# Graph attention, mix and experts on one core: table counts, first edge maxima and the exponentials of k moved into the projections

## The chip, the cores and the metric

The kernel runs on one core of a Trainium2 chip, as one launch. The metric is the device time of that launch in microseconds (us); lower is better. Executions of the kernel before took 1727.99, 1735.38 and 1739.04 us.

## What is computed

x has 1250 nodes of 768 features; the graph has 21,250 edges and a loop at each node. Three parts follow each other: a graph network, a linear attention ("the mix") and a mixture of experts. All inputs of the first two come from LayerNorm(x) or a first linear layer of it.

```
gat_conv (3 layers, H = 4 heads, C = 192):
    h = (x1 @ W).reshape(N, H, C)
    e = leaky_relu((h * a_src).sum(-1)[src] + (h * a_dst).sum(-1)[dst], 0.2)
    m = segment_max(e, dst);  p = exp(e - m[dst]);  s = segment_sum(p, dst)
    out = segment_sum((p / s[dst])[:, :, None] * h[src], dst)
mix (12 heads of 64, 256 features):
    data_dash = (64 ** -0.25 * data) @ proj.T
    q' = ratio * (exp(data_dash - diag - max over its own features) + EPS)
    k' = ratio * (exp(data_dash - diag - max over all heads, nodes, features) + EPS)
    out = q' (k'^T v) / (q' . sum k')
```

What matters for the change: the maximum under the exponential of k is one number over everything, so k' can't be finished before the last product of k is known; and the softmax over edges is worked densely, on a table of 1250 x 1250 counts (how often an edge u to v occurs), so that no edge is gathered.

## The kernel before

**Order.** A generator, `whole_order`, yields all steps of the program as one list cut into ticks, and each engine runs its own part of each step in that order (SP issues most of the DMAs, POOL the scatters). The engines are held together by semaphores only. `paced` lets tracks run side by side: a track with rate 0.5 puts one of its steps into every second tick. Within the second part two tracks of rate 1 run side by side: `projection_steps` followed by `mix_steps`, and `graph_steps`.

**First part.** LayerNorm, the first linear layer (x1) and h of three layers on TensorE. Meanwhile VectorE makes, in groups of eight chunks, the places and amounts of 170 chunks of 125 edges, and POOL (`place_`, L2043) adds each chunk into a table in DRAM with an indirect DMA. There are two tables, used in turn, because a scatter must wait until the last one into the same table has landed. Both are filled with zeros at the start (L2018).

**Projections** (`projection_steps`). v is made in 20 ticks; then come 36 products in two ticks each: for each of six pairs of heads the k rows (n even, c = 0 to 2) and the q rows (n odd), in columns of 512, 512 and 226. One half of a product is nine matmuls. During the q products of a pair `k_top` (L968, L1366) forms data_dash of that pair's k, tile by tile (three matmuls of 512 columns, `dash_into`, into banks 4 and 5 in turn), and VectorE takes its maximum. The product is then thrown away. `qk_split` puts k and q as two bf16 parts into an SBUF row, and `qk_store` writes it to DRAM. top_max, top_turn and top_spread give the maximum of all to every partition, and k_shift = -(diag + top).

**Graph** (`graph_steps`). It waits until the projections are over. Then come the counts (rate 0.6 a tick, ten tiles): SP loads a row block of both tables (L2155), VectorE adds them and the loops (L1387), ScalarE copies to bf16, TensorE transposes it (`count_turn`, L985), and VectorE makes `absent` (L1396), -3e38 where there is no edge. Then the 40 `edge_max` steps of layer 0 (L1408, rate 1.1 a tick; four heads x ten tiles), and `shifts` (L1418), which goes through DRAM to be spread to all partitions by `head_in` (L2187). Only then the attention begins: 120 items at 0.5 a tick, each `edge_z` (VectorE), `edge_exp` (ScalarE), `weigh` (VectorE), `gather` (20 matmuls, TensorE); beside it the 80 edge maxima of layers 1 and 2 at 0.6 a tick.

**Mix** (`mix_steps`). For each of six pairs 10 ticks of k tiles, 10 of q tiles, 3 empty ones: `dash` (L1018, three matmuls), then for k `k_exp` (L1887: two Exp with bias k_shift, and a Relu that adds EPS) and `k_sum` (L1027), for q `q_exp`, `q_turn`, `q_feat`, `q_out`, `divide`. After it come the output products of the mix and of the three layers (`row_block`), each layer's as soon as its attention is through, then the experts.

The waits that the prediction speaks of, before the change:

```
pe.wait_ge("k_max", i - 1)                # k_top(i): the maximum two tiles back is taken
sy.wait_ge("scatter0", 16 * (CHUNKS - CHUNKS // TABLES))   # SP, first load of a table: all scatters
ve.wait_ge(f"shift_in{lh % 2}", 32 * (lh // 2 + 1))        # edge_z: head_in's rows have landed
ve.wait_ge("gather_mm", i - EDGE_BUFFERS + 1)
```

## Time and profile before

| | us |
|---|---|
| three runs | 1727.99, 1735.38, 1739.04 (median 1735.38) |
| profiled execution | 1733.43 |
| its span, from the first to the last instruction | 1731.7 |
| TensorE busy (matmuls) in the span | 1569.7 (91%) |
| VectorE busy | 1121.2 (65%) |
| ScalarE busy | 682.0 (39%) |
| POOL busy | 411.0 (24%) |

The profile is of one execution. The span leaves out 1.7 us of the execution's own time. Busy times are unions of instructions; a matmul's end is modelled, and a busy TensorE can still issue faster or slower, so rates are read from the starts of successive instructions. PEclk is the share of full speed that TensorE's clock was granted.

### The profile page before, as it was taken

Reading aid. Unit: us, or ns where it says so; the run is one execution under the profiler, and the core shown is the slowest. Engines: PE = TensorE matmul, PEld = TensorE weight load, DVE = VectorE, ACT = ScalarE, POOL = GpSimd, SP = SyncE. Lnnn points to the kernel's source line nnn. Section 1 sums busy time; section 2 is a strip of 40 time slices with the busy share of each in tenths; the row PEclk is TensorE's granted clock in tenths of the full one; section 3 lists DMA queues with packets and bytes.
Section 4 is the critical chain, followed back from the end, with each engine's and each line's share of the span. In section 5 each row is a group of like instructions: output and inputs, shape, how many; then the busy total and the mean of one; then the engine's idle time right before and its main releaser. Section 6 shows DMA issues by size and latency. Waiting matters only on the chain.

```text
span 1731.7 us, 24915 instructions
## 1 busy us (share of the span) xinstructions
PE 1569.7 (91%) x9670; PEld 1195.3 (69%) x9731; DVE 1121.2 (65%) x2563; ACT 682.0 (39%) x1359; POOL 411.0 (24%) x250
## 2 busy tenths in 40 slices
PE   3979999999997888799999899989999999986987
PEld 2556666556654666689888788878889886665664
DVE  6678664114343597878778999968667753885233
ACT  4421000122222776667777543446334522441110
POOL 3777777768740000000000000000000000002331
PEclk9999999999998998899999899998999999996999
DMA  9234534453522422514212534444123214645951
GB/s 345 21 66 112 118 82 112 70 100 56 130 52 104 161 90 77 170 35 141 76 38 80 186 112 148 140 164 142 63 80 111 96 40 145 229 178 193 319 156 53
DMA packets 192568, 207.41 MB, mean 120 GB/s; under 512 B 80801, under 2 KB 149039, under 8 KB 192450
## 3 DMA queue, kind: packets, MB, share of 16 engines
q1 hardware_dynamic: 116354, 183.88, 32.2%
q0 software_dynamic: 75232, 19.57, 7.7%
q10 hardware_dynamic: 864, 2.36, 0.4%
q8 instruction: 77, 1.26, 0.3%
q14 instruction: 41, 0.34, 0.1%
HBM read 141.62 MB, written 65.27 MB: 119 GB/s over the span
## 4 chain that ended last, share of the span: by engine, by line
PE 74%; DVE 14%; ACT 5%; DMA 3%; issue 3%; SPq 1%; POOLq 0%; POOL 0%; ACTq 0%; DVEq 0%
PE bank L1012 19%; PE bank L858 13%; PE bank L859 13%; PE bank L857 12%; PE bank L1181 4%; PE bank L1169 3%; PE bank L1037 2%; DVE junk L1414 2%; PE bank L1065 2%; DVE eb L1451 2%; DVE eb L1460 1%; ACT ef L1883 1%; PE bank L959 1%; PE bank L1080 1%; DVE q_max L1483 1%
## 5 line engine op out<-in xcount | busy, mean ns | idle before, releaser
L1012 PE MATMUL bank<-hb,eb 128*128 128x193 f32 (+3 forms) x2400 | 419.7, 332 | 26.8 <-DVE eb L1460 21.8
L1012 PEld LDWEIGHTS bank<-hb,eb 128*128 128x128 f32 (+3 forms) x2400 | 401.1, 191 | 37.9 <-DVE eb L1460 24.8
L2049 POOL DMA_INDIRECT table<-amount,place x170 | 347.2, 2042 | 120.8 <-DMA table<-amount,place 71.9
L2055 POOL IOTA iota8i<- 128x8 int32 x1 | 0.1, 140 | 940.9 <-DMA node_rows<-node 940.9
L1844 ACT ACTIVATE eb<-eb,asd 128x640 f32<-128x640 f32 (+1 forms) x240 | 181.6, 812 | 54.9 <-DVE eb L1451 54.9
L1451 DVE SCALAR_TENSOR_TENSOR eb<-shift_b,as_low,shift_b 128x640 f32<-128x640 f32 (+1 forms) x240 | 196.3, 859 | 6.9 <-DMA shift_b<-shift_rows 6.8
L1460 DVE SCALAR_TENSOR_TENSOR eb<-eb,count 128x1280 f32<-128x1280 f32 (+1 forms) x120 | 174.3, 1453 | 6.4 <-ACT eb L1844 6.2
L1414 DVE CUSTOM_DVE_ANT_0 junk<-ab,absent 128x1250 bf16<-128x1250 f32 x120 | 174.3, 1453 | 1.3
L857 PE MATMUL bank<-wg_hi,x1T_hi 128*128 128x384 bf16 (+3 forms) x360 | 118.7, 330 | 0.5 <-DVE x1T_lo L1283 0.5
L857 PE MATMUL bank<-w_o_hi,aT_hi 128*128 128x384 bf16 (+1 forms) x360 | 118.6, 330 | 0.0
L859 PE MATMUL bank<-w_o_hi,aT_lo 128*128 128x384 bf16 (+1 forms) x360 | 118.5, 329 | 0.0
L859 PE MATMUL bank<-wg_hi,x1T_lo 128*128 128x384 bf16 (+3 forms) x360 | 118.5, 329 | 0.0
L858 PE MATMUL bank<-wg_lo,x1T_hi 128*128 128x384 bf16 (+3 forms) x360 | 118.5, 329 | 0.0
L858 PE MATMUL bank<-w_o_lo,aT_hi 128*128 128x384 bf16 (+1 forms) x360 | 118.5, 329 | 0.0
L1297 DVE TENSOR_TENSOR h_row<-bank,bgr 128x384 f32<-128x384 f32 (+1 forms) x60 | 32.4, 555 | 64.5 <-PE bank L859 64.3
L1883 ACT ACTIVATE ef<-bank,q_shift 128x256 f32<-128x256 f32 (+1 forms) x120 | 50.6, 477 | 59.8 <-DVE q_shift L1488 59.7
L858 PE MATMUL bank<-xnT_lo,wq_hi 128*128 128x512 bf16 (+1 forms) x210 | 70.8, 337 | 3.5 <-DVE wq_lo L1259 2.7
L859 PE MATMUL bank<-xnT_hi,wq_lo 128*128 128x512 bf16 (+1 forms) x216 | 73.0, 338 | 0.3
L1716 DVE TENSOR_TENSOR orow<-bank,b2r 105x384 f32<-105x384 f32 (+1 forms) x32 | 17.8, 555 | 84.5 <-PE bank L1181 84.5
L1369 DVE TENSOR_REDUCE kmax<-bank 128x1 f32<-128x512 f32 (+1 forms) x60 | 40.2, 692 | 49.1 <-PE bank L859 49.1
L1824 ACT ACTIVATE sq<-bank 128x512 f32<-128x512 f32 (+1 forms) x36 | 18.7, 519 | 130.0 <-PE bank L859 130.0
L857 PE MATMUL bank<-xnT_hi,wq_hi 128*128 128x512 bf16 (+1 forms) x204 | 68.6, 336 | 0.0
(286 smaller groups left out, 2945.8 us busy)
## 6 DMA issues: line engine op xcount, KB each, us to landing
w<-in_w SPq DMA_DIRECT2D x16, 1152.0 KB, 12.6
shift_b<-shift_rows SPq DMA_DIRECT2D x24, 625.0 KB, 5.9
h_rows<-h_row SPq DMA_DIRECT2D x27, 388.0 KB
hb<-h_rows SPq DMA_DIRECT2D x12, 873.0 KB
ar<-node_rows SPq DMA_DIRECT2D x27, 384.0 KB, 3.2
qk_rows<-qk_row SPq DMA_DIRECT2D x12, 625.0 KB
ab<-as_rows SPq DMA_DIRECT2D x12, 625.0 KB, 5.8
stage<-in_W SPq DMA_DIRECT2D x18, 384.0 KB, 4.2
```

What stands on the lines that cost most here:

```text
L857: T.matmul(out_ap, lhs[0], rhs[0], start=first, stop=False, skip_group_check=skip)
L858: T.matmul(out_ap, lhs[0], rhs[1], start=False, stop=False, skip_group_check=skip)
L859: return T.matmul(out_ap, lhs[1], rhs[0], start=False, stop=last, skip_group_check=skip)
L1012: ins = T.matmul(bank[w // 2][0:M, c0:c0 + GC + 1], p[0:K, u, w * P:w * P + M], hv[0:K, t, 0:GC + 1], start=opens and u == 0 and w % 2 == ...
L1169: ins = T.matmul(bank[i % 2][:, 0:CAP], w1s[e % WEIGHT_SETS][:, k, f * 128:(f + 1) * 128], sT_of(k)[:, e * CAP:(e + 1) * CAP], start=k == ...
L1181: ins = T.matmul(bank[4 + i % 4][0:r1 - r0, 0:HROWS], hT[e % 2][:, f, r0:r1], w2s[e % WEIGHT_SETS][:, f, cs], start=f == 0, stop=f == KF - 1)
L1414: V.tensor_tensor_reduce(out=junk[0:R, :], in0=ab[lh % 2][0:R, :], in1=absent[0:R, t, :], scale=1.0, scalar=-BIG, op0=ALU.add, op1=ALU.max ...
L1451: ins = V.scalar_tensor_tensor(eb[i % EDGE_BUFFERS][:, u, 0:w], low, as_low[:, t, lh:lh + 1], high, ALU.add, ALU.max)
L1460: V.scalar_tensor_tensor(e, e, 1.0, count[:, 2 * pair:2 * pair + 2, ns], ALU.min, ALU.mult).then_inc(sem["edge_w"], 1)
L1844: ins = A.activation(e[:, u, 0:w], e[:, u, 0:w], ACT.Exp, bias=asd[:, t, 8 * l + hh:8 * l + hh + 1])
L1883: ins = A.activation(ef[g % 4][0:R, hh, :], bank[3 + g % 2][0:R, hh * FEATS:(hh + 1) * FEATS], ACT.Exp, bias=bias)
L2049: G.indirect_dma_start(tables[i], bass.IndirectOffsetOnAxis(place[:, c:c + 1], axis=0), amount16[:, c:c + 1], None, compute_op=ALU.add).th ...
```

## The change

- **Third table.** TABLES is 3. The first eight chunks go to tables 0 and 1, later ones to the three in turn. The third is filled with zeros by POOL just ahead of the first scatter. The counts load three row blocks per tile and add twice.
- **Counts in the projections.** At product 17 of 36 the graph's track may start: one count tile in every second tick, then the edge maxima of layer 0 at 0.75 a tick until the projections end, and at 1.1 after. The transposes of counts now use banks 6 and 7. The first attention item stands 29 ticks earlier in the order than before.
- **Exponentials of k kept.** After each k_top VectorE also negates the tile's row maxima (kneg), ScalarE takes exp(data_dash - own maximum) of 128 x 512 into one of three e_out buffers (`k_keep`), and SP stores it to e_rows in DRAM. k_top(i) waits for k_kept (the Exp two tiles back) where it waited for k_max. Behind the top, k_shift becomes exp(own maximum - diag - top). In the mix there is no dash for k: SP loads the kept tile (`e_load`, five buffers, issued four steps ahead), ScalarE applies the scale and EPS with two Relus, and k_sum reads it.

```diff
-TABLES = 2
+TABLES = 3
+AHEAD, RING = 4, 5
-COUNT_RATE, FIRST_EDGE_RATE, EDGE_RATE, ATTENTION_RATE = 0.6, 1.1, 0.6, 0.5
+COUNTS_AT = 17
+COUNT_RATE, EARLY_EDGE_RATE, FIRST_EDGE_RATE, EDGE_RATE, ATTENTION_RATE = 0.5, 0.75, 1.1, 0.6, 0.5
...
+def table_of(c):
+
+    return c % 2 if c < CP else c % TABLES
...
     def product(m):
         n, c = divmod(m, NC)
+        if m == COUNTS_AT:
+            done.add("scattered")
...
+            yield from (("k_keep", i) for i in unkept)
+            unkept.clear()
             if n % 2 and 2 * c + part:
                 for t in range(4 * c + 2 * part - 2, 4 * c + 2 * part):
                     yield "k_top", NT * (n // 2) + t
+                    unkept.append(NT * (n // 2) + t)
...
 def graph_steps(done):
+    while "scattered" not in done:
+        yield None
+    yield "ab_in", 0
+    yield from paced((in_step([(2, lambda t: [("count_turn", t), ("absent", t)]), (1, lambda t: [("count", t)]),
+                               (0, lambda t: [("tab_in", t)])], NT), COUNT_RATE))
+    yield from spread(edge_layer(0), lambda: FIRST_EDGE_RATE if "projected" in done else EARLY_EDGE_RATE)
     while "projected" not in done:
         yield None
-    yield from paced((in_step([(1, lambda t: [("count_turn", t)]), (0, lambda t: [("count", t)]),
-                               (1, lambda t: [("absent", t)])], NT), COUNT_RATE))
-    yield "ab_in", 0
-    yield from paced((edge_layer(0), FIRST_EDGE_RATE))
...
             def k_top(i):
...
-                pe.wait_ge("k_max", i - 1)
+                pe.wait_ge("k_kept", i - 1)
...
                 V.tensor_reduce(kmax[0:R, i:i + 1], bank[4 + i % 2][0:R, :], AX.X, ALU.max).then_inc(sem["k_max"], 1)
+                ve.wait_ge("k_max", 2 * i + 1)
+                V.tensor_scalar(kneg[0:R, i:i + 1], kmax[0:R, i:i + 1], -1.0, None, ALU.mult).then_inc(sem["k_max"], 1)
...
                 V.tensor_tensor(count[:, t, :], tb[0][:, :], tb[1][:, :], ALU.add).then_inc(sem["counted"], 1)
-                ve.wait_ge("counted", 2 * t + 1)
+                ve.wait_ge("counted", TABLES * t + 1)
+                V.tensor_tensor(count[:, t, :], count[:, t, :], tb[2][:, :], ALU.add).then_inc(sem["counted"], 1)
...
+            def k_keep(i):
+                R = rows(i % NT)
+                if i < 3:
+                    se.wait_ge(f"h_out{i}", 16 * (NT * LAYERS // 3))
+                se.wait_ge(f"e_out{i % 3}", 16 * (i // 3))
+                se.wait_ge("k_max", 2 * i + 2)
+                A.activation(e_out[i % 3][0:R, :], bank[4 + i % 2][0:R, :], ACT.Exp,
+                             bias=kneg[0:R, i:i + 1]).then_inc(sem["k_kept"], 1)
...
+            def k_feat(pair, t):
...
+                se.wait_ge("k_scale", 1)
+                se.wait_ge(*kept_in(n))
                 for hh in range(2):
...
+                    ins = A.activation(e[0:R, hh, :], e[0:R, hh, :], ACT.Relu, bias=eps[0:R, :],
+                                       scale=k_shift[0:R, t, 2 * pair + hh:2 * pair + hh + 1])
+                ins.then_inc(sem["k_feat"], 1)
...
             def place_(q):
-                ge.wait_ge("table_zero", 16 * TABLES)
+                if q == 0:
+                    G.dma_start(tables[2].rearrange("(p t n) o -> p t (n o)", p=P, n=TABLE[1]),
...
+            def k_keep(i):
+                pair, t = divmod(i, NT)
+                sy.wait_ge("k_kept", i + 1)
+                S.dma_start(e_rows[pair, at(t), :], e_out[i % 3][0:rows(t), :]).then_inc(sem[f"e_out{i % 3}"], 16)
...
+            def e_load(n):
+                sy.wait_ge("qk_mm", NC * 2 * PAIRS)
+                if n >= AHEAD + RING:
+                    sy.wait_ge("feat_used", used(n - RING, "k"))
+                load_kept(n)
```

**Where instructions stand.** TensorE at the head of the mix, before (`top`: the last step of the global maximum; `k_first`: k of pair 0; `ef`: its exponentials; `count`: a tile of counts in bf16):

```order
L982 MATMUL bank<-top,ones 128x1
L857 MATMUL bank<-feats_hi,k_first 128x512
L858 MATMUL bank<-feats_lo,k_first 128x512
L859 MATMUL bank<-feats_hi,k_first 128x512
L857 MATMUL bank<-feats_hi,k_first 128x512
L858 MATMUL bank<-feats_lo,k_first 128x512
L859 MATMUL bank<-feats_hi,k_first 128x512
L1037 MATMUL bank<-v_first,ef_211 128x65 x4
L857 MATMUL bank<-feats_hi,k_first 128x512
L858 MATMUL bank<-feats_lo,k_first 128x512
L859 MATMUL bank<-feats_hi,k_first 128x512
L994 MATMUL bank<-ident_61,count_0_147 128x128 x9
```

The same place after (`e_first`, `ek`: kept tiles loaded from DRAM; L1099 is k_sum):

```order
L1042 MATMUL bank<-top,ones 128x1
L1099 MATMUL bank<-v_first,e_first_153 128x65 x4
L1099 MATMUL bank<-v_first,e_first_154 128x65 x4
L1099 MATMUL bank<-v_first,e_first_155 128x65 x4
L1099 MATMUL bank<-v_first,e_first_156 128x65 x4
L1099 MATMUL bank<-v_first,ek_131 128x65 x4
```

A k tile has no product of its own left there, and the transposes of counts are gone from between the tiles.

VectorE in the q products of a pair, before (`kmax`: maxima of k_top; `diag`, `qk_row`: norms and the low part of q):

```order
L1369 TENSOR_REDUCE kmax<-bank 128x1 x2
L1361 TENSOR_SCALAR diag<-bank 128x2
L1361 TENSOR_SCALAR diag<-bank 98x2
L1351 SCALAR_TENSOR_TENSOR qk_row_193<-bank,qk_row_193 128x512
L1369 TENSOR_REDUCE kmax<-bank 128x1 x4
L1361 TENSOR_SCALAR diag<-bank 128x4x2
```

After, in the fourth pair's q products, where the counts run:

```order
L1430 TENSOR_REDUCE kmax<-bank 128x1
L1432 TENSOR_SCALAR kneg<-kmax 128x1
L1430 TENSOR_REDUCE kmax<-bank 128x1
L1432 TENSOR_SCALAR kneg<-kmax 128x1
L1471 TENSOR_SCALAR absent<-bank 128x8x128
L1471 TENSOR_SCALAR absent<-bank 128x128
L1471 TENSOR_SCALAR absent<-bank 98x128
L1458 TENSOR_TENSOR count<-tab_148,tab_149 128x1250
L1460 TENSOR_TENSOR count<-count,tab_150 128x1250
L1462 TENSOR_TENSOR count<-count,ident 128x128
L1422 TENSOR_SCALAR diag<-bank 128x2
```

Each maximum has a negation behind it, and a count tile (three absents, three adds) stands between one pair of maxima and the next.

## Rows read from the trace of the kernel before

**Rows 1.** Busy time by stretch: us, then PE, PEld, DVE, ACT, POOL (instructions), PEclk, DMA, GB/s

```profile
374.00:551.00 177.00, 175.11 (x1050) 106.83 (x1068) 75.23 (x154) 41.51 (x83) 97.85 (x48) 1.00 0.36 78
551.00:698.00 147.00, 115.46 (x771) 85.89 (x783) 99.55 (x202) 100.26 (x215) 0.00 (x0) 0.89 0.39 129
698.00:945.00 247.00, 229.45 (x1519) 207.90 (x1544) 204.59 (x317) 178.43 (x389) 0.00 (x0) 0.98 0.27 88
945.00:1114.00 169.00, 157.71 (x951) 137.41 (x950) 166.19 (x229) 78.15 (x148) 0.00 (x0) 0.96 0.44 145
1114.00:1434.00 320.00, 308.90 (x1913) 266.60 (x1911) 218.33 (x293) 140.19 (x252) 0.00 (x0) 0.98 0.30 97
```

**Rows 2.** Timeline of VectorE in the head of the mix: start, us busy

```profile
636.71 0.68 DVE L1483 TENSOR_REDUCE q_max<-bank 128x2 f32<-128x512 f32 x1
637.42 0.16 DVE L1488 SCALAR_TENSOR_TENSOR q_shift<-q_max,diag 128x2 f32<-128x2 f32 x1
637.50 1.45 DVE L1414 CUSTOM_DVE_ANT_0 junk<-ab,absent 128x1250 bf16<-128x1250 f32 x1
```

**Rows 3.** Timeline of ScalarE, the end of k in pairs 1, 2 and 5

```profile
636.17 0.39 ACT L1909 ACTIVATE context<-bank 128x260 f32<-128x260 f32 x1
...
686.76 0.39 ACT L1909 ACTIVATE context<-bank 128x260 f32<-128x260 f32 x1
...
914.92 0.41 ACT L1909 ACTIVATE context<-bank 128x260 f32<-128x260 f32 x1
```

**Rows 4.** Timeline of ScalarE in the head of the mix, the Relu of a k tile

```profile
621.65 0.72 ACT L1892 ACTIVATE ef<-ef,eps 128x512 f32<-128x512 f32 x1
```

**Rows 5.** Timeline of VectorE, the first shift step and the first edge_z

```profile
685.91 0.21 DVE L1424 TENSOR_TENSOR mz<-m_col,asd 128x40 f32<-128x40 f32 x1
...
697.94 1.68 DVE L1451 SCALAR_TENSOR_TENSOR eb<-shift_b,as_low,shift_b 128x640 f32<-128x640 f32 x2 [6.76 <-DMA shift_b<-shift_rows]
```

**Rows 6.** Timeline of TensorE, k tiles beside the attention

```profile
818.47 0.38 PE L857 MATMUL bank<-feats_hi,kT 128*128 128x512 bf16 x1
...
819.12 3.43 PE L1012 MATMUL bank<-hb,eb 128*128 128x193 f32 x20
822.39 1.00 PE L1037 MATMUL bank<-vs,ef 128*128 128x65 f32 x8
...
825.67 3.43 PE L1012 MATMUL bank<-hb,eb 128*128 128x193 f32 x20
```

**Rows 7.** Groups by line, VectorE's work for the attention: busy us, mean ns

```profile
L1451 DVE SCALAR_TENSOR_TENSOR eb<-shift_b,as_low,shift_b 128x640 f32<-128x640 f32 (+1 forms) x240 | 196.3, 859 | 6.9 <-DMA shift_b<-shift_rows 6.8
L1460 DVE SCALAR_TENSOR_TENSOR eb<-eb,count 128x1280 f32<-128x1280 f32 (+1 forms) x120 | 174.3, 1453 | 6.4 <-ACT eb L1844 6.2
```

**Rows 8.** Timelines of TensorE and VectorE, one tile of counts

```profile
591.62 0.72 PE L994 MATMUL bank<-ident,count 128*128 128x128 bf16 x10
...
592.26 0.95 DVE L1402 TENSOR_SCALAR absent<-bank 128x1024 bf16<-128x1024 bf16 x3 [0.87 <-PE bank L994]
...
593.93 0.80 DVE L1391 TENSOR_TENSOR count<-tab,tab 128x1250 uint16<-128x1250 uint16 x1
```

**Rows 9.** Timeline of VectorE, maxima of k_top at the products of 226 columns

```profile
399.79 1.34 DVE L1369 TENSOR_REDUCE kmax<-bank 128x1 f32<-128x512 f32 x2 [0.78 <-PE bank L859]
401.95 1.34 DVE L1369 TENSOR_REDUCE kmax<-bank 128x1 f32<-128x512 f32 x2 [0.83 <-PE bank L859]
```

**Rows 10.** Landing of stores: of node rows (KB, us), and of v rows (390 KB)

```profile
node_rows<-node SPq DMA_DIRECT2D x12, 480.0 KB, 2.8
...
DMA to landing us min/median/max: 3.9/4.2/5.0
```

**Rows 11.** POOL's scatters: line, waits before them, and the zero fills' landing

```profile
L2049 POOL DMA_INDIRECT table<-amount,place x170: 1984/1991/2778, 47.0 to 500.4; - x170
...
  DMA table<-amount,place: 71.9, 53
...
DMA to landing us min/median/max: 16.6/20.5/24.3
```

More of the change, by code:

```diff
@@ L128, in paced, with spread @@
                     break
+        yield None
+def spread(steps, rate):
+    due = 0.0
+    while True:
+        due += rate()
+        while due >= 1:
+            due -= 1
+            for step in steps:
+                if step is None:
+                    break
+                yield step
+            else:
+                return
         yield None
@@ L1477, in q_exp @@
                 R = rows(t)
-                g = dash_of(pair, "q", t)
                 q = NT * pair + t
```

181 lines of the change are left out of this document (108 added, 73 removed), and 6 rows, old and new, of the table TAKEN_OVER.

## The prediction

> **What bounds the kernel now.** I read three things in this order: the busy time by stretch, the timelines of each engine inside the stretches that the change touches, and the landing times of DMAs. All work stands in one order made of ticks, so I count in ticks: the number of ticks between two steps follows from the rates in the code, and the trace gives what a tick costs. By stretch [rows 1]: the projections (374 to 551) keep TensorE busy for 175.1 of 177 us while VectorE has 75.2 and ScalarE 41.5. Then come 147 us (551 to 698) in which no engine is full: PE 115.5 at a granted clock of 0.89, DVE 99.6, ACT 100.3. They hold the counts, two and a half pairs of the mix and the 40 edge maxima of layer 0, and the attention cannot begin before they are through. From 698 to 945 mix and attention share PE (229.5 of 247); from 945 to 1114 DVE is the bound (166.2 of 169), and from 1114 to 1434 PE again (308.9 of 320). So the place with slack is 551 to 698, and the projections have slack on DVE and ACT only.
>
> **Part 1: the head of the mix.** Before, the first attention item (edge_z 0) stands 63 ticks behind top_max: 20 for the counts at 0.6 a tick, 38 for 41 edge steps at 1.1, the rest the head's steps. After, counts and 10 of the 40 edge maxima stand in the projections, and it is 34 ticks. What these cost: an edge maximum keeps DVE busy for 1.45 us (I take 1.5 with the read of its result), a q tile for 0.79 from its maximum to what follows [rows 2]. In the 25 ticks up to the shifts stand 27 edge maxima (41 us) and a q part (10 tiles and 5 reciprocals, 9 us), 50 us of DVE; one pair of the same content took 50.6 us for 23 ticks [rows 3], with about 47 of DVE in it, so I take 55. ScalarE is no bound there: it loses the Exp of k, and its one Relu on 512 columns, 0.72 us [rows 4], becomes two on 256 columns with a scale from a tile. The trace has no such Relu; bounds for the two are 0.72 and 1.44, I take 0.85, and a k tick of over 2 us hides either. The top chain adds 2 us. From the first shift step to the first edge_z passed 12.0 us [rows 5], nearly all DMA; now six ticks of k tiles lie inside it, and I leave it at 12. Sum 69 us in place of 146.7: **-78**.
>
> **Part 2: what was moved beside the attention.** 29 more ticks of the mix now run beside it: 12 k tiles, 14 q tiles, 3 empty. A pair beside the attention took (914.9-686.8)/3 = 76.0 us [rows 3]. Two k ticks took 6.55 us, from 819.12 to 825.67 [rows 6]: 3.27 for one gather, twice 0.65 for a dash (818.47 to 819.12), and the two k_sum with short waits in the 1.98 left. The dash of k is gone, so PE needs 2.6 us a k tick. DVE needs there, per two ticks, 2x0.86+1.45 for an attention item [rows 7], its reciprocals, and 1.2 edge maxima (1.8), that is 2.6 a tick: the two are level. Bounds: 2.6 (PE alone) and 3.05 (169 us for the 55 ticks of the stretch where DVE is full); I take 2.7. The other 13 ticks of a pair cost (76.0-32.8)/13 = 3.32. So the moved ticks cost 12x2.7 + 17x3.32 = 89, and the 30 k tiles that stood there before give back 30x0.58 = 17: **+72**.
>
> **Part 3: behind the mix.** The attention ends 29 ticks earlier in the order, which is 14.5 items less beside the row blocks. PE is the bound there, so each gives back its gather of 3.27 us [rows 6]: **-47**. The third row block then runs alone, with PE as full as before.
>
> Parts 1 to 3 together: -53. Of this PE's own work explains 39 (60 dashes of 0.65) and 7 (the transposes of the counts, moved); the rest is idle time.
>
> **Part 4: what the projections pay.** PE is full there, so whatever is late for PE or added to it counts.
> - 100 transposes of counts: at most 0.72 us for ten [rows 8]: +7.
> - DVE gets ten counts (two adds of 0.80, one of 0.3) and the absents (0.95) [rows 8], 2.9 us for each product, 60 negations (0.16 each, as the small q_shift of [rows 2]) and ten edge maxima. For a product with four k_top that is 7.2 to 7.9 us beside 7.1 (512 columns) or 5.1 (226 columns) of PE. In the fourth q projection DVE falls behind by some 2 us, in the last by some 4, when an edge maximum stands between two pairs of kmax. Elsewhere it catches up: +6. Bounds 0 and 15.
> - k_top(i) used to wait for a maximum two tiles back, now for an Exp two tiles back. Maxima of neighbouring pairs start 2.2 us apart at the narrow products [rows 9]; from the dash's end to a free bank it is now 0.69+0.16+0.72 and some 0.5 for four hand-overs, about 2.1 us, and for the pair's second 2.8: a stall of 0.7 to 1 us for each of the six q projections. Behind the waiting dash PE's next product is queued.
> - Exp i waits for the store of i-3. A turn of that ring is 0.72 (Exp), 0.1, 0.35 (SP's issue) and the landing L. Ten tiles span three turns, beside 12.6 us now. L of 256 KB is not in the trace: 480 KB stores landed in 2.8 us, 390 KB ones in 3.9 to 5.0 [rows 10]. With 2.8 the ring costs nothing, with 3.5 1.4 us, with 5.0 5.9 us for ten tiles. I take 3.5, and 5 while the tables load beside it (some 1 MB a product). Ring and stall overlap: together +12. Bounds 4 and 40.
>
> "DMA: Bandwidth & Descriptors" (Anatomy of one DMA) of the Trainium skill gives a DMA about 2.0 us fixed, most of it the receipt of the write and worst where the target is HBM, plus bytes over 436 GB/s: an estimate of 2.6 us by that page, and a ring that costs nothing. The 390 KB rows stand at 3.9 to 5.0, so here the trace is the more pessimistic, and by the page alone the sum would end some 6 us lower.
>
> **Do the counts find their tables?** The 170 scatters start at 47.0 and end at 500.4 [rows 11], 71.9 us of it waiting for a table's last scatter. With three tables that wait goes and 0.3 us of issue stands for each of 53: -56. Against it stands the third fill, issued ahead of the first scatter: a fill of 3 MB takes some 8 us (the two of before landed 16.6 and 24.3 us behind their issues), so the third scatter, which needs the first, starts some 6 us late. End: 500+4-56+7 = 455. SP reaches the first table load at tick 105, which is 374+17.7/36x177 = 461. It is met with 6 us to spare, and DVE comes for the data a whole product later. In "DMA: Bandwidth & Descriptors" (Queues, rings and completion order) each DMA engine takes a ring's descriptors in ring order, the HWDGE rings at least; that makes the first scatters wait for the whole fill, as I have it. If they overtook it, the end would be 449, and nothing in the sum would change.
>
> **Sum.** -53 + 7 + 6 + 12 = -28, and +2 for k loads that come late behind the loads of a head. The profiled execution took 1733.4 us (span 1731.7), so 1707; it lies 2 us under the median of the three runs, 1735.4, and with half of that the forecast is **1708**.
>
> **Rivals.**
> 1. *The mix does not get faster* (0.18). DVE sets the k ticks at 3.05, the figure of the stretch where it is full. For it: PE's 2.6 and DVE's 2.6 leave neither a reserve. Against it: DVE had only 204.6 of 247 us. 42 k ticks by 0.35 are +15: 1723.
> 2. *The projections hide nearly everything* (0.12): L is 2.8, DVE's backlog drains under the k projections. Toll 10 in place of 25: 1692.
> 3. *The ring paces the projections* (0.12), the case on the other side. Place: e_out and banks 4 and 5, with the k_top of all six q projections. Each us of L adds 3 us to each, 18 in all. From L = 6.1 the kernel is slower by over 1%: the gain of 53, less 13 for the first two tolls, is 40, and 6x(3x(6.1+1.17)-12.6) is 55. At 6.5: 62, so 1757. For it: table loads, weight loads, k and q stores and these stores make about 2.5 MB a product of 7.8 us, as dense as the chip moved anything here. Against it: only one of the six projections has the tables beside it.
> 4. *It doesn't do what it says* (within case 1 or 3): the scatters end after 470, SP stands at the table load and DVE at the first count, with qk_lo queued behind and PE two products later. Each us then costs one; it needs 10 us more than I have.
>
> **How the numbers follow.** The forecast has 0.58. A change of over 1% (17 us, about what a measurement of this kernel tells from none) begins at 1718: of the forecast 0.52 lies below and 0.06 within 1%. Rival 1 gives 0.02 faster and 0.16 same, rival 2 0.12 faster, rival 3 0.03 same and 0.09 slower. Together 0.66, 0.25, 0.09. Range: the low end is rival 2 with k ticks at 2.6, 1688; the high end takes rival 1 and a toll 15 above mine, 1738.
>
> **What would show it.** Right: the last scatter near 450; the first attention item 75 to 80 us earlier before the toll, so at 640 to 650; the projections' end at 570 to 580; two k ticks beside a gather in 5.4 us; PE waiting at k_top for ScalarE, 1 to 2 us for each q projection. Wrong: projections that end after 600, waits of the e_out Exp for DMA of over 2 us each, or k ticks that stay at 3.2 with PE waiting for the edges' DVE work.

## The result, and the profile after

The changed kernel took 1728.51 us (median of 20 runs, 1720.02 to 1732.28), the kernel before 1734.43 us (20 runs, 1727.99 to 1740.21). The ratio is 0.996, with a 95% interval of 0.9948 to 0.9972: 0.4% faster, where 1708 was forecast with a range of 1688 to 1738. The time lies inside the range, but the forecast was faster by over 1% with a chance of 0.66, and it is a change within 1%.

The profiled execution (1724.5 us, 4 under the median) has a span of 1722.8 us where the kernel before had 1731.7. Both spans can be cut at the same four instructions: VectorE's first reduction over all k maxima (L1436 `top<-kmax`, the projections' end), the first edge_z, the last shift of a q tile, the end.

```
                         before    after    difference   forecast (Parts 1 to 4)
projections' end          551.2    599.4      +48.2        +25
... to first edge_z       146.7     72.5      -74.2        -78
... to last q_shift       246.6    316.8      +70.2        +72
... to the end            787.2    734.0      -53.2        -47, and +2 for late k loads
sum                      1731.7   1722.8       -8.9        -26
```

Three of four terms came out within 2, 4 and 8 us. The fourth, the toll in the projections, is twice its size and took what the other three gave. Busy time by stretch, the columns of [rows 1]:

```profile
374.00:600.00 226.00, 194.34 (x1149) 114.57 (x1169) 124.53 (x298) 93.97 (x155) 63.13 (x32) 0.94 0.58 180
600.00:672.00 72.00, 59.76 (x304) 52.75 (x307) 55.69 (x100) 38.18 (x90) 0.00 (x0) 0.64 0.43 138
672.00:989.00 317.00, 295.91 (x1995) 276.51 (x2011) 282.18 (x435) 226.78 (x496) 0.00 (x0) 0.97 0.39 123
989.00:1067.00 78.00, 62.66 (x360) 58.56 (x360) 71.92 (x100) 41.44 (x80) 0.00 (x0) 0.93 0.42 136
1067.00:1400.00 333.00, 329.59 (x2054) 280.64 (x2053) 235.20 (x322) 145.84 (x265) 0.96 (x6) 0.99 0.35 115
```

Before, the projections kept TensorE busy for all but 1.9 us. Now it idles for 31.7 of 226 us, and neither VectorE (125) nor ScalarE (94) comes near to being full: nothing is overloaded, so the engines must be waiting for each other. Against [rows 11], the scatters now end at 447.2, with 8.5 us of waits on a table in place of 71.9, earlier than the 455 of the sum. That sum charged some 7 us for the third fill. The fill was issued at 34.3 us, 13.5 us ahead of the first scatter, and the third scatter came at 54.0 where it came at 51.8 before; whether a scatter waits for a fill doesn't show here:

```profile
L2133 POOL DMA_INDIRECT table<-amount,place x170: 1988/1993/2737, 47.8 to 447.2; - x170
```

Who waited for whom between 374 and 600 us, from the view of the waits (engine and line, what it waited for, us in total, times, longest):

```profile
ACT count L1901 <- DVE count L1462: 47.3, 10, 7.0
...
ACT e_out L1945 <- DVE kneg L1432: 28.2, 24, 2.2
DVE qk_row L1412 <- ACT qk_row L1896: 22.9, 17, 2.2
PEld bank L916 <- ACT e_out L1945: 21.1, 16, 4.7
...
PE bank L916 <- ACT e_out L1945: 15.3, 10, 4.4
...
PE bank L1054 <- ACT count L1901: 8.4, 4, 3.6
...
DVE count L1458 <- DMA tab<-table: 5.7, 2, 4.5
...
ACT e_out L1945 <- DMA e_rows<-e_out: 2.8, 4, 1.2
```

The first line is the one to look at. L1901 is ScalarE's copy of a count tile to bf16: before each of its ten copies ScalarE stands still, for 4.7 us on average. The last line speaks against the ring of stores (rival 3): only 2.8 us of waits for stores of e_rows in all. ScalarE's own timeline at the third and fourth copy (start, us busy, and in brackets the idle time before it):

```profile
480.91 1.25 ACT L1901 ACTIVATE count<-count 128x1250 bf16<-128x1250 uint16 x1 [3.51 <-DVE count L1462]
482.06 0.58 ACT L1892 ACTIVATE sq<-bank 128x512 f32<-128x512 f32 x1
482.54 0.59 ACT L1896 ACTIVATE qk_row<-bank 128x512 bf16<-128x512 f32 x1
486.64 1.25 ACT L1901 ACTIVATE count<-count 128x1250 bf16<-128x1250 uint16 x1 [3.51 <-DVE count L1462]
...
494.50 1.25 ACT L1901 ACTIVATE count<-count 128x1250 bf16<-128x1250 uint16 x1 [5.39 <-DVE count L1462]
495.65 0.58 ACT L1892 ACTIVATE sq<-bank 128x512 f32<-128x512 f32 x1
496.12 0.59 ACT L1896 ACTIVATE qk_row<-bank 128x512 bf16<-128x512 f32 x1
496.60 1.27 ACT L1945 ACTIVATE e_out<-bank,kneg 128x512 f32<-128x512 f32 x2
```

and VectorE's beside it:

```profile
483.16 0.69 DVE L1412 SCALAR_TENSOR_TENSOR qk_row<-bank,qk_row 128x512 bf16<-128x512 f32 x1 [2.21 <-ACT qk_row L1896]
483.77 0.95 DVE L1471 TENSOR_SCALAR absent<-bank 128x1024 bf16<-128x1024 bf16 x3
484.63 0.80 DVE L1458 TENSOR_TENSOR count<-tab,tab 128x1250 uint16<-128x1250 uint16 x1
485.46 0.81 DVE L1460 TENSOR_TENSOR count<-count,tab 128x1250 uint16<-128x1250 uint16 x1
486.31 0.29 DVE L1462 TENSOR_TENSOR count<-count,ident 128x128 uint16<-128x128 uint16 x1
...
490.77 0.15 DVE L1432 TENSOR_SCALAR kneg<-kmax 128x1 f32<-128x1 f32 x1
```

Read them as one circle. The copy (480.91) stands ahead of the split of a product (sq 482.06, qk_row 482.54). VectorE's half of that split (483.16) stands ahead of the absents (483.77) and the next count (484.63), and the next copy (486.64) waits for that count. Once round is 1.15 + 1.10 + 0.61 + 0.86 + 2.01 = 5.73 us, of which ScalarE stands idle for 3.51 and VectorE for 2.21, and it must be gone through once for each product. With maxima and a weight split in it, it was 7.86 us (486.64 to 494.50). Before, six products took TensorE 30 us, 5 on average. The k maxima hang on the circle too: the kneg of 490.77 was ready, but its Exp stood behind the copy at 494.50 and came at 496.60. TensorE, which waits for that bank:

```profile
493.15 0.38 PE L918 MATMUL bank<-xnT_hi,wq_lo 128*128 128x512 bf16 x1
497.35 0.61 PE L916 MATMUL bank<-feats_hi,qk_row 128*128 128x512 bf16 x1 [3.82 <-ACT e_out L1945]
...
510.29 0.61 PE L916 MATMUL bank<-feats_hi,qk_row 128*128 128x512 bf16 x1 [4.40 <-ACT e_out L1945]
```

This larger circle, through TensorE's k_top, the maxima and their Exp behind the next copy, costs more than the one of 5.73 us. By the starts of ScalarE's squares, the two products of the fourth q projection with four k_top each (22 and 23) last 12.93 and 12.21 us where they lasted 6.79 and 5.14: 13.2 us of lag from two products. The three k products that last one round of 5.73 us (19, 20 and 26) lasted 4.20, 2.55 and 2.55 before: 7.9 us.

After the 3.82 us of idleness the same matmul takes 0.61 where it took 0.38: by the profile the granted clock fell to the lower of its two levels (1.2 GHz; the mean is 0.50 from 497.5 to 500.0), and the matmuls stayed slow for some 3 us. Over 460 to 599 its mean is 0.90, where [rows 1] show 1.00 for the projections. What that costs: TensorE was busy for 112.2 us from 460 to 599; before it was 90.0 from 460 to 551, the transposes add 7.2, and some 5 us of work were still ahead of it at 460 (the lag of then, 4.2 us at product 16 and 5.4 at 17). An estimate from these figures gives the 10 us left over to matmuls at the lower clock. So 48 us of toll are some 10 of slow clock, 7 of transposes and about 30 of waits.

When did the lag arise? ScalarE's square of product m, after minus before: 2.2 us at product 0, where the two executions differ before the first k_top, 4.2 at product 16 (k_top and the exponentials alone), 5.4 at 17, then 15.0 at 20, 31.4 at 23, 42.4 at 27, and 45.2 at the last, 35. The ten counts stand at products 17 to 27. So 37 of the 48 us arise there, and little in the q projections before and behind them.

What the terms rested on, in the trace after. TensorE's k ticks beside the attention, against [rows 6]:

```profile
875.39 3.49 PE L1073 MATMUL bank<-hb,eb 128*128 128x193 f32 x20
878.71 1.90 PE L1099 MATMUL bank<-vs,ek 128*128 128x65 f32 x16
880.45 3.49 PE L1073 MATMUL bank<-hb,eb 128*128 128x193 f32 x20
883.77 1.90 PE L1099 MATMUL bank<-vs,ek 128*128 128x65 f32 x16
885.50 3.49 PE L1073 MATMUL bank<-hb,eb 128*128 128x193 f32 x20
```

Two k ticks and a gather now take 5.06 us (875.39 to 880.45), with no wait of TensorE in the rows, where 5.4 were forecast and 6.55 were taken before.

### The profile page after: what moved, and what is told of

It is laid out like the page before. It is cut to its first block, busy times and chain, and to the rows that moved or that the text cites. A ratio compares the mean times of both kernels' runs of the same rounds, so it can differ in the third digit from the quotient of the medians.

```text
span 1722.8 us, 24788 instructions
## 1 busy us (share of the span) xinstructions
PE 1552.3 (90%) x9504; PEld 1191.6 (69%) x9551; DVE 1136.6 (66%) x2634; ACT 691.2 (40%) x1360; POOL 408.7 (24%) x251
## 3 DMA queue, kind: packets, MB, share of 16 engines
q8 instruction: 75, 1.23, 0.3%
## 4 chain that ended last, share of the span: by engine, by line
PE 70%; DVE 18%; ACT 4%; DMA 3%; issue 3%; SPq 1%; POOLq 0%; POOL 0%; ACTq 0%; DVEq 0%
PE bank L1073 19%; PE bank L917 12%; PE bank L918 11%; PE bank L916 11%; PE bank L1242 4%; DVE junk L1483 3%; PE bank L1230 3%; PE bank L1099 3%; PE bank L1126 3%; DVE eb L1520 1%; DVE eb L1529 1%; PE bank L1141 1%; PE bank L1111 1%; PE bank L926 1%; DVE q_max L1551 1%
## 5 line engine op out<-in xcount | busy, mean ns | idle before, releaser
L2133 POOL DMA_INDIRECT table<-amount,place x170 | 343.5, 2020 | 70.6 <-issue 48.8
L1959 ACT ACTIVATE ek<-ek,eps,k_shift 128x256 f32<-128x256 f32 (+1 forms) x112 | 58.9, 600 | 34.4 <-DMA ek<-e_rows 34.4
L916 PE MATMUL bank<-xnT_hi,wq_hi 128*128 128x512 bf16 (+1 forms) x207 | 72.1, 348 | 0.3 <-issue 0.2
L1858 ACT ACTIVATE wg_hi<-stage 128x776 bf16<-128x776 f32 x18 | 15.3, 850 | 135.6 <-DVE stage L1334 125.2
## 6 DMA issues: line engine op xcount, KB each, us to landing
w<-in_w SPq DMA_DIRECT2D x16, 1152.0 KB, 14.4
```

The costliest lines, as they stand in the source:

```text
L916: T.matmul(out_ap, lhs[0], rhs[0], start=first, stop=False, skip_group_check=skip)
L1959: ins = A.activation(e[0:R, hh, :], e[0:R, hh, :], ACT.Relu, bias=eps[0:R, :], scale=k_shift[0:R, t, 2 * pair + hh:2 * pair + hh + 1])
L2133: G.indirect_dma_start(tables[i], bass.IndirectOffsetOnAxis(place[:, c:c + 1], axis=0), amount16[:, c:c + 1], None, compute_op=ALU.add).th ...
```

## The experiments

Four theories of the 23 us that the toll is over its forecast. **A**: ScalarE's copy of a count stands ahead of a product's split, which makes the circle shown. **B**: VectorE has too much to do once it has the counts. **C**: the exponentials of k, their wait for room and their stores stall TensorE. **D**: the DMA queues are too full for the table loads. In the kernel each step name of the order runs a piece on every engine that has a function of that name, so "count" is VectorE's adds and ScalarE's copy, in one place of the order. The kernel before stood at 1736.6 to 1738.2 us beside these runs (the medians of the four groups of runs); ratios are to it, with their 95% intervals. Where projections' ends are compared, two things scatter from execution to execution: each stands on one profiled execution, and the lag at product 0, before any k_top, lies between -1.8 and 4.4 us.

**1. The work on k alone.** Counts and edge maxima go back behind the projections.

```diff
-    while "scattered" not in done:
-        yield None
-    yield "ab_in", 0
-    yield from paced((in_step([(2, lambda t: [("count_turn", t), ("absent", t)]), (1, lambda t: [("count", t)]),
-                               (0, lambda t: [("tab_in", t)])], NT), COUNT_RATE))
-    yield from spread(edge_layer(0), lambda: FIRST_EDGE_RATE if "projected" in done else EARLY_EDGE_RATE)
     while "projected" not in done:
         yield None
+    yield from paced((in_step([(1, lambda t: [("count_turn", t)]), (0, lambda t: [("tab_in", t), ("count", t)]),
+                               (1, lambda t: [("absent", t)])], NT), 0.6))
+    yield "ab_in", 0
+    yield from paced((edge_layer(0), FIRST_EDGE_RATE))
...
```

(In the lines left out the transposes use banks 1 and 2 again and wait for the last product.)

> The changed kernel with the counts, absents and first edge maxima put back behind the projections (rates 0.6 and 1.1); the exponentials of k and their stores stay in the projections, and so does the third table. Theory A (the toll of the projections comes from the step of a count, whose copy by ScalarE stands ahead of that product's own split and exponential) and theory B (VectorE has too much to do once it carries the counts): the projections end at 555 to 562 us where the changed kernel has 599.4 and the kernel before 551.2, and the first edge_z comes at about 700 again. Theory C (the exponentials of k, their wait for room and their stores are what stalls TensorE): they still end at 580 us or later. Whole, by A and B: the head costs its 147 us again and the pairs beside attention keep their 68, so about 1725 to 1735 by the changed kernel's 50 us behind the mix plus what the mix gains; by C 20 us more.

1727.05 us, ratio 0.9937 (0.9921 to 0.9954). Projections' end 555.5: a toll of 4.3 (5.8 from product 0 on, where this execution led by 1.5), and theory C falls as a cause by itself. The head took 166.2 us, not 147, and the first edge_z came at 721.7, not at about 700: the table loads stand in the tick of their count, and this view of the waits from 556 to 722 us shows both sides waiting for loads. That miss is of this kernel's making and says nothing of the changed one.

```profile
DVE count L1455 <- DMA tab<-table: 18.7, 3, 10.3
...
ACT ek L1956 <- DMA ek<-e_rows: 12.9, 8, 3.3
```

**2. The counts and edge maxima alone.** The kernel before with the third table and with the order of the changed one for counts and edges; the mix keeps the dash and the Exp of k.

```diff
-TABLES = 2
+TABLES = 3
...
-    while "projected" not in done:
+    while "scattered" not in done:
...
+    yield from paced((in_step([(2, lambda t: [("count_turn", t), ("absent", t)]), (1, lambda t: [("count", t)]),
+                               (0, lambda t: [("tab_in", t)])], NT), COUNT_RATE))
...
```

> The kernel before with the third table and with counts, absents and first edge maxima in the projections from product 17 on; no exponentials of k there, k dash is made in the mix as before. It tells how much of the toll is there without the work on k. Theory A (the copy of a count stands ahead of the split on ScalarE; the exponentials only lengthen that chain): half or more of it stays, the projections end at 575 to 590. Theory B (VectorE's own load: counts and absents alone are about 2.1 us a product more, with kneg 0.5 on top): 585 to 599. Theory C (the work on k is the cause, the counts only its company): 555 to 562. The head afterwards should last 72 to 76 us from the projections' end to the first edge_z, and the pairs beside attention 76 again.

1730.55 us, 0.9951 (0.9935 to 0.9967). Projections' end 576.5, a toll of 25.3: inside what A expected (575 to 590), near its low end, and below B's 585 to 599; the head took 74.2 us and a pair beside the attention 75.0 ((961.5-736.5)/3 by the ends of k), as expected or near it (76). The circle is there without the work on k:

```profile
ACT count L1871 <- DVE count L1431: 50.1, 10, 7.8
```

The tolls of 1 and 2 add up to 29.6, and together in the changed kernel they are 48.2. The exponentials of k stand in the same queue behind the copy, which would lengthen the circle; products 22 and 23 last 8.58 and 9.99 us here, 12.93 and 12.21 with them.

**3. The copy one product later.** The same instructions on each engine; ScalarE's copy becomes a step of its own (`count_copy`), behind the split and the Exp that it stood ahead of, and transposes and absents move with it. So two things move; experiments 4 and 9 take them apart.

```diff
-    yield from paced((in_step([(2, lambda t: [("count_turn", t), ("absent", t)]), (1, lambda t: [("count", t)]),
-                               (0, lambda t: [("tab_in", t)])], NT), COUNT_RATE))
+    yield from paced((in_step([(3, lambda t: [("count_turn", t), ("absent", t)]), (2, lambda t: [("count_copy", t)]),
+                               (1, lambda t: [("count", t)]), (0, lambda t: [("tab_in", t)])], NT), COUNT_RATE))
...
```

> The changed kernel, but ScalarE's copy of a count tile stands one product later, behind the split and the exponential of the product that it stood ahead of; its transposes and absents one later still. Same instructions on every engine. Theory A: the splits no longer wait for a count, the toll of 38 us in the stretch of the counts falls to 10 to 20, the projections end at 570 to 580, and the whole is 15 to 28 us faster than the changed kernel (1700 to 1713). Theory B (VectorE's load): nothing moves, projections' end 595 to 603, whole within 4 us of 1728. Theory D (the DMA queues, density of stores and table loads): nothing moves either.

1701.08 us, 0.9775 (0.9752 to 0.9798): 27 us faster than the changed kernel by the medians, on the fast side of what theory A expected. (The profiled executions differ by 22.4 us of span: that of the changed kernel was one of its shorter ones, that of this kernel its longest.) Projections' end 572.3. It is called kernel 3 below. VectorE has the same load, so B falls as the cause; DMA engines were busier (0.66 of 460 to 572, 229 GB/s, against 0.54 and 188 from 460 to 599 in the changed kernel), so D falls as the cause of these 27 us too. The waits from 374 to 600 us, with the lines of the changed kernel:

```profile
ACT count L1901 <- DVE count L1462: 13.8, 7, 3.4
...
PE bank L916 <- ACT e_out L1945: 6.6, 10, 1.5
...
ACT e_out L1945 <- DMA e_rows<-e_out: 4.6, 5, 1.4
...
DVE qk_row L1412 <- ACT qk_row L1896: 2.9, 8, 0.6
```

All three waits of the circle are much smaller: 47.3 became 13.8, 22.9 became 2.9, and TensorE's wait for a bank 15.3 became 6.6. TensorE no longer waits for the copy (8.4 us in the changed kernel). The granted clock from 460 to 572 is 0.99.

**4. The copy on GpSimd,** which has nothing to do after its last scatter.

```diff
+            def count_(t):
+                ge.wait_ge("counted", TABLES * (t + 1))
+                ge.wait_ge("count_turned", 2 * (t - 1))
+                G.tensor_copy(count16[t % 2][:, :], count[:, t, :]).then_inc(sem["count_copied"], 1)
...
```

> The changed kernel, but GpSimd makes the copy of a count tile in place of ScalarE; what VectorE and TensorE do is the same. Theory A: ScalarE loses ten copies of 1.24 us and the wait for VectorE ahead of each (47 us in all), so the splits start as soon as their product is there; projections' end 565 to 580 and the whole 15 to 30 us faster than the changed kernel, unless GpSimd's copy is so slow (over 6 us) that the transposes of a count wait for it. Theory B: VectorE has the same load, nothing moves by more than 4 us.

1709.33 us, 0.9828 (0.9806 to 0.9851), projections' end 579.8: the second way of taking the copy out of the split's way gives 19 us. GpSimd needs 1.23 us for a copy, as ScalarE does. It is less than in 3, and the transposes were not put off here, so that TensorE still waits for the copy itself, from 460 to 580 us (experiment 9 puts them off):

```profile
PE bank L1054 <- POOL count L2177: 5.5, 3, 2.5
```

**5. The counts alone, with the copy later:** the edit of 3 on the kernel of 2.

> The counts without the work on k, as in the second experiment, but with ScalarE's copy one product later. Theory A (the loop through ScalarE's queue) says that here too the copy held up the split: of the 25 us that the counts cost the projections, 10 to 17 go, projections' end at 560 to 567. Its rival A2, that the copy only hurts where the exponentials of k stand behind it as well, says 573 to 577 as before. What stays is then the price of VectorE's own work and of the 100 transposes (7.1 us).

1719.42 us, 0.9884 (0.9853 to 0.9915), projections' end 562.1: of the toll of 25.3, 14.4 went. From product 17 to 35 the lag grows from 0.9 to 7.4 us, by 6.5, and the 100 transposes cost TensorE 7.2. So up to the last product the counts cost TensorE no more than their transposes, once the copy is out of the way. The projections' end comes 3.5 us later still (10.9), because on VectorE three edge maxima of 1.45 us stand between the last k maximum and the reduction. ScalarE still waits 22.2 us ahead of the copies (50.1 in 2), and the projections lose little by it. Rival A2 falls.

**6. Less for VectorE.** The add of the third table is left out, 0.81 us less for each count; the edges counted in that table are missing from the output.

```diff
-                V.tensor_tensor(count[:, t, :], tb[0][:, :], tb[1][:, :], ALU.add).then_inc(sem["counted"], 1)
-                ve.wait_ge("counted", TABLES * t + 1)
-                V.tensor_tensor(count[:, t, :], count[:, t, :], tb[2][:, :], ALU.add).then_inc(sem["counted"], 1)
+                V.tensor_tensor(count[:, t, :], tb[0][:, :], tb[1][:, :], ALU.add).then_inc(sem["counted"], 2)
```

> The kernel with the copy one product later, and VectorE's add of the third table left out (so the output lacks the edges of that table): one instruction of 0.81 us less for each count. If what is left of the toll in the stretch of the counts (13 us) is VectorE's load, 4 to 8 us of it go and the projections end at 564 to 568 in place of 572.3. If it is only waits of the hand-overs and the transposes, they end at 571 to 573.

1701.21 us, 0.9778 (0.9747 to 0.9810), projections' end 576.5. It came to product 17 with a lag of 5.7 us, 2.2 more than kernel 3, before any count; from there to the last product it lost 16.3 where kernel 3 lost 14.2. Eight us less of VectorE's work, of some 29 for the counts, gave nothing where 4 to 8 were expected if its load were what is left of the toll.

**7. Count and absents apart.** Two halves of a product in place of one block.

```diff
+    def of(*names):
+        return lambda i: [(name, i // 2) for name in names if i % 2 == 0]
+
+    yield from in_step([(5, of("count_turn", "absent")), (4, of("count_copy")), (2, of("count")), (0, of("tab_in"))],
+                       2 * NT - 1)
```

> The kernel with the copy one product later, and the transposes and absents of a count in the other half of the product from the count itself, so that VectorE never has both (1.9 and 0.95 us) in one block ahead of a product's split; the same instructions. If the size of the block counts: the projections end at 565 to 569 in place of 572.3 and the whole is 2 to 6 us faster than the 1701 of that kernel. If it is VectorE's load as a sum: 571 to 574, no difference.

1704.62 us, 0.9822 (0.9788 to 0.9857), projections' end 573.8: no difference that can be told from kernel 3, so the size of the block shows no effect. It is not a clean test: VectorE waits 11.5 us for table loads here (7.2 in kernel 3), and ScalarE 7.7 for stores of e_rows, up to 3.4 for one (4.6 and 1.4), which could hide a small gain.

**8. More edge maxima in the projections:** `EARLY_EDGE_RATE` 1.25 in place of 0.75, on kernel 3.

> The kernel with the copy one product later, and edge maxima of layer 0 at 1.25 a tick in place of 0.75 behind the counts: 16 of 40 stand in the projections in place of 9 or 10. In the last k projection VectorE has room (its lag there was 2 us): the head of the mix loses six edge maxima of 1.45 us. If the head is bound by VectorE: 4 to 8 us faster than 1701, first edge_z at 642 to 646. If the head is bound by the number of ticks of the mix in it, the gain is the same or a little more, as 5 ticks leave it; what speaks against is a toll of 2 to 4 us in the last projection, since a k_top waits there for an edge maximum: whole 1695 to 1701.

1709.51 us (1705.02 to 1721.14), 0.9859 (0.9814 to 0.9905), projections' end 577.2 and first edge_z 636.1: the attention begins 14 us earlier and the kernel is not faster. The head lost 18.9 us against kernel 3, the stretch to the last q_shift gained 18.7. The expectation was wrong: the projections lost 4.9 us, and the ticks of the mix that leave the head are paid beside the attention at nearly the same price.

**9. GpSimd's copy, and the transposes one product later:** kernel 4 with lag 3 in place of 2 for "count_turn" and "absent".

> GpSimd makes the copy of a count tile, as in the fourth experiment, and now the transposes and absents stand one product later too, so that TensorE has no reason to wait for it. ScalarE has neither the ten copies (12.4 us) nor their wait for VectorE. If the harm came from the wait ahead of the split alone: the same as the kernel with ScalarE's copy one product later, projections' end 570 to 574, whole 1698 to 1705. If ScalarE's own 1.24 us for each copy count too, or its spare time shortens the chain to k_top: projections' end 560 to 568, whole 5 to 10 us less. If it is slower than that kernel (as the fourth was, 1709), GpSimd's copy slows VectorE beside it.

1699.12 us (1692.81 to 1707.08), 0.9791 (0.9757 to 0.9825), projections' end 572.4, the same as kernel 3 and 7.4 less than experiment 4. ScalarE has 11.4 us less to do from 460 to 572 us (43.3 against 54.7) and nothing comes of it: the harm was in where the copy stood, not in its 1.24 us. With experiment 4 it also splits the gain of 3: of 27.1 us of projections some 20 are the copy's leaving ScalarE's queue ahead of the split, some 7 the later transposes.

**10. No edge maxima in the projections:** `EARLY_EDGE_RATE` 0 on kernel 3.

> The kernel with the copy one product later, and no edge maxima in the projections: all 40 of layer 0 stand in the head of the mix, at 1.1 a tick. It tells what the third thing moved, the first edge maxima, is worth. By ticks: nine more ticks of mix ahead of the first edge_z, head 78 + 9x2 to 9x3 = 96 to 105, of which 1.5 to 2 us come back in the projections and part beside the attention. By the last run (six more edge maxima early: head 19 us shorter, all of it given back between the first edge_z and the last q_shift): the whole moves by less than 5 us, 1700 to 1706. Rival: the head is where the time goes, 1712 to 1720.

1696.09 us (1691.76 to 1699.81), 0.9756 (0.9723 to 0.9788). First edge_z 663.1, 13 us later than in kernel 3, and yet no slower (1700 to 1706 was expected). The head took 90.2 (96 to 105 expected), the stretch to the last q_shift 287.9 in place of 315.5, the rest 744.0 in place of 734.7. With 8 it says: on top of the other two things moved, the first edge maxima brought nothing.

**11. Kernel 3 again,** beside 9 and 10.

> The third experiment again, on the chip of its two neighbours, for a comparison with them and a narrower interval: 1701, ratio to the kernel before 0.976 to 0.980.

1701.61 us (6 runs), 0.9798 (0.9763 to 0.9833), projections' end 574.6. Its interval overlaps that of 10, so the 5 us between them are not shown.

**12. 9 and 10 together.**

> The two last edits together: GpSimd's copy with transposes and absents one product later, and no edge maxima in the projections. If both gains are there and independent (the first some 2 us by the medians, the second some 5), 1692 to 1698; if they are within the scatter of the measurement, the same as either, 1696 to 1701. Projections' end at 571 to 574 either way, head 86 to 91, a ratio to the kernel before of 0.972 to 0.979.

1697.65 us (5 runs), 0.9791 (0.9768 to 0.9814). The gains do not add up. Kernels 3, 9, 10 and 12, at 1696 to 1702, can't be told apart. Their medians are 1.6 to 1.9% below the changed kernel's, and 2.0 to 2.4% below the kernel before; the intervals of all of them together reach from 1.7 to 2.8%.

The stretches of all of them, as in the first table (us), with the lag behind the kernel before at products 0, 17 and 35:

```
                         proj. end  to edge_z  to q_shift  to end   lag 0  lag 17  lag 35
before                     551.2      146.7      246.6     787.2       0       0       0
after                      599.4       72.5      316.8     734.0     2.2     5.4    45.2
1  work on k alone         555.5      166.2      214.6     782.3    -1.5     2.9     4.6
2  counts alone            576.5       74.2      339.4     734.2    -0.8    -0.8    22.0
5  2, copy later           562.1       79.3      343.2     734.5     1.3     0.9     7.4
3  after, copy later       572.3       77.9      315.5     734.7    -0.7     3.5    17.7
6  3, one add less         576.5       78.1      312.3     735.7     2.4     5.7    22.0
7  3, absents apart        573.8       66.9      325.0     736.5    -0.1     4.4    19.2
8  3, six maxima more      577.2       59.0      334.2     732.9     2.2     5.4    20.3
10 3, no maxima early      572.8       90.2      287.9     744.0    -1.8     4.2    21.9
4  copy on GpSimd          579.8       73.3      318.1     741.8     1.1     4.5    25.8
9  4, transposes later     572.4       74.1      312.2     731.9    -0.7     3.4    17.8
11 3 again                 574.6       77.8      312.3     735.7     4.4     6.5    20.0
12 9, no maxima early      570.4       90.2      285.1     750.6     2.9     5.9    19.4
```

## Why the prediction was wrong

**Right: Part 1.** The head was to shrink by 78 us to 69 and shrank by 74.2 to 72.5. The first edge_z was forecast for 640 to 650 and came at 671.9, which is the toll's doing: in kernel 3 it comes at 650.2.

**Right: Part 2.** +72 was forecast and +70.2 measured, with k ticks of 2.53 us (half of 5.06) where I took 2.7 and gave 2.6 as the lower bound, and the pair beside the attention at 68.2 us ((960.8-756.1)/3 by the ends of k in the profile after). Rival 1, k ticks at 3.05, didn't happen.

**Right in kind: Part 3.** -47 was forecast, -53.2 measured; where the other 6 us come from was not followed. The +2 for late loads of k belongs to the stretches before this one: the waits from 600 to 1000 us (columns as above) have them.

```profile
ACT ek L1959 <- DMA ek<-e_rows: 34.4, 9, 13.2
...
PE bank L1099 <- ACT ek L1959: 9.9, 2, 9.3
```

TensorE lost 9.3 us to one of them, which ended at 682 us and so is part of the 70.2 above: the +2 was too small. Without that wait Part 2 would be some 61, 11 under its forecast, of which the 42 k ticks at 2.53 in place of 2.7 explain 7. That +72 and +70.2 lie so near each other is in part luck.

**Wrong: Part 4.** The step that failed is its list. It charges the counts with 100 transposes and with VectorE's adds and absents, and has no line for ScalarE's part of a count, the copy at L1901: 12.5 us of an engine with much room, which I took as free without naming what stood behind it in its queue. Its place, between one product's count and that product's split, costs 27 us with the transposes that wait for it (48.2 in the changed kernel, 21.1 with copy and transposes one product later), some 20 of it in ScalarE's queue (28.6 with the copy on GpSimd). It was to be read beforehand: the order puts the "count" of a tick behind the projection's steps of that tick, and so ahead of the split of the next, on all engines at once.

Term by term, against kernel 3, where the copy is out of the way:
- Transposes, +7: right, 7.2 us busy, and 6.5 of lag in experiment 5.
- VectorE's backlog, +6 (bounds 0 and 15): 3.4, and in another place than the sum had it. The lag at the last square is 17.7 and the projections' end comes 21.1 late; the 3.4 between are the edge maxima ahead of the reduction (3.5 in experiment 5, and none in experiment 10, which has no edge maxima there). That anything else of the backlog reached TensorE isn't shown: experiment 6 found nothing.
- k_top's stall and the ring, together +12 (bounds 4 and 40): alone they cost 6.1 from product 0 to 35 (experiment 1, lag -1.5 to 4.6). That is the upper end of the 4.2 to 6 us by which the prediction priced the stall alone, with nothing for the ring: stores were waited for 4.9 us in all there (2.8 in the changed kernel, 4.6 in kernel 3), none for more than 1.6.
- In no term: from product 17 to 35 the lag grows by 14.2 in kernel 3, where the counts alone give 6.5 and the work on k alone 1.7 (2.9 to 4.6). Some 6 us more arise only where the two share the products. That the stall, the ring and these 6 add up to the forecast's 12 is luck.
- "DMA: Bandwidth & Descriptors" (Anatomy of one DMA) of the Trainium skill led to the estimate of a ring that costs nothing. The short waits agree with it better than with my bounds from the 390 KB stores. The section fits DMAs that GpSimd issues, though, and SP issues these stores, whose landing no view here gives.
- Their sum, 25, stands against a toll of 21.1 in kernel 3, and the forecast of 1708 against its 1701. So the size was nearly right for a kernel in which the copy stood elsewhere, by terms of which one was right, one was half its size, and one hit its sum by another way.

**The rivals.** Rival 3, the one on the other side, named the right place (the banks of k_top, for which TensorE waits 15.3 us) and the wrong resource: it watched DMA, and its sign of e_out waiting for DMA over 2 us each did not come, the longest being 1.2. The sign of a waiting k_top was forecast at 1 to 2 us for each q projection: it is 1.1 in kernel 3 (6.6 in all), and 2.6 in the changed kernel. "Projections that end after 600" was given as what would make it wrong, and at 599.4 it was all but met. Rival 4 fell with the scatters' end at 447.2; two table loads were waited for, 5.7 us in all.

**How much each part of the change is worth,** with the copy moved: counts and edge maxima without the work on k 12.6 us of span (experiment 5), the work on k 18.7 on top of it (kernel 3: 10.2 more of toll, 27.7 less beside the attention). Without the work on k's company, early counts as written gave 7.4 and the work on k alone 13.1; together they gave 8.9. The circle took the rest. These are spans of single executions, while runs of one kernel differ by 7 us and more.

**What stays open.** Some 6 us of toll arise only where counts and exponentials of k share the products; 8 us less of VectorE's work, the size of its block and ScalarE's copy time were tried and made no difference. Two causes are left. One is the shared wait of k_top for an Exp behind both: TensorE still waits 6.6 us for e_out in kernel 3 (4.4 with the work on k alone). The other is what is left of theory D: VectorE waits 7.2 us for table loads in kernel 3 and 0.3 in experiment 5, where the DMA engines moved 158 GB/s from 460 to 562 us and not 229. No run takes the two apart. Why the first edge maxima bring nothing was not followed either; the stretches show only where it is given back.

## What to carry to other kernels

When a step is moved beside a tight loop, list its instruction on every engine, the cheap ones on the idle engines above all, and write beside each what stands behind it in that queue. A short copy that waits for another engine's fresh result, put ahead of that engine's next input, closes a circle that runs at the sum of the steps on both engines (5.73 us here, with both idle for part of it); one position later in the order was enough here to open it. The sign in this profile is a group of waits between two engines of which neither is full, in both directions (47.3 us of ScalarE for VectorE and 22.9 of VectorE for ScalarE). The first of them alone is none: with the copy later ScalarE still waits 22.2 us in experiment 5, and little is lost by it.

## What was unexpected of the hardware

A stall of TensorE costs more than its own length here: after 3.82 us of waiting, a matmul of 512 columns took 0.61 us in place of 0.38 for some 3 us more, and by the estimate above such windows added some 10 us to the toll. GpSimd's copy of 128x1250 from uint16 to bf16 took 1.23 us, no longer than ScalarE's 1.24. ScalarE's Relu with its scale and bias from tiles took 600 ns on 256 columns where [rows 4] show 0.72 us for 512, and two behind each other start 0.49 us apart, so a pair takes 1.1 us where 0.85 was assumed; the k ticks of 2.53 us hid it.
